# A decoder layer with latent attention and two expert stages on one core: low halves ahead of router steps, values copied first on ScalarE, unread products moved behind the attention loop, three normalisations on VectorE

## The reference, cut to what matters

```python
x = x + attn(layernorm(x))        # 8 heads, keys and values from 32 compressed features, softmax over 64 tokens
x = x + moe1(layernorm(x), ctx)   # router on ctx: best 2 of 8 experts per token, 128 -> 512 -> 128, relu
x = x + moe2(layernorm(x))        # 32 small experts, best 8 of 32, silu gate, and a shared expert
```

## Time and profile before

| | us |
|---|---|
| median of 3 runs (lowest to highest) | 756.46 (754.01 to 759.85) |
| the profiled execution's own time | 756.52 |
| its span, first to last instruction | 754.8 |
| PE busy in the span | 669.3 (89%) |
| DVE busy | 552.5 (73%) |
| POOL busy | 345.7 (46%) |
| ACT busy | 353.1 (47%) |

### The profile page before, as it was taken

The page is one execution under the profiler, slowest core; times in us unless marked ns, Lnnn a source line. Parts: engine busy times, 40 slices in busy tenths (PEclk is TensorE's granted clock), DMA queues, the critical chain, the costliest instruction groups (busy, mean ns, idle before and its releaser), DMA issues.

```text
span 754.8 us, 11001 instructions
## 1 busy us (share of the span) xinstructions
PE 669.3 (89%) x3456; PEld 475.5 (63%) x3456; DVE 552.5 (73%) x1318; ACT 353.1 (47%) x628; POOL 345.7 (46%) x386
## 2 busy tenths in 40 slices
PE   6868999999708999999992988999999999999997
PEld 5535666666506777777771755666666666666664
DVE  4367877779517999999964786777868695958564
ACT  3844666655204666666663533444343424353221
POOL 5111377778867999999957324040312213000000
PEclk9967999999958999999997898999999999999999
DMA  9900300000023466666311293354555545444442
GB/s 227 366 11 0 92 30 29 29 29 34 38 77 88 127 206 193 179 188 193 113 56 45 59 207 87 90 154 109 132 112 138 129 112 132 111 130 112 124 116 58
DMA packets 73816, 84.14 MB, mean 111 GB/s; under 512 B 15057, under 2 KB 42683, under 8 KB 73758
## 3 DMA queue, kind: packets, MB, share of 16 engines
q1 hardware_dynamic: 68536, 74.93, 36.4%
q0 software_dynamic: 4096, 8.40, 3.8%
q10 hardware_dynamic: 1126, 0.11, 0.1%
HBM read 64.48 MB, written 18.87 MB: 110 GB/s over the span
## 4 chain that ended last, share of the span: by engine, by line
PE 57%; POOL 18%; DVE 11%; issue 7%; ACT 4%; DMA 2%; another core or an unknown queue 0%; SPq 0%; POOLq 0%; ACTq 0%; DVEq 0%
PE pair_banks L1625 15%; POOL h1h L586 7%; PE bank L1408 7%; PE bank L1410 6%; PE bank L1409 6%; POOL W2l L571 4%; PE pair_banks L1315 4%; PE score_banks L1410 3%; PE score_banks L1408 3%; PE score_banks L1409 3%; POOL W2h L566 3%; PE bank L1447 2%; PE pair_banks L1493 2%; POOL x_sorted L544 2%; PE bank L1467 2%
## 5 line engine op out<-in xcount | busy, mean ns | idle before, releaser
L865 ACT ACTIVATE r_s<-bank 128x512 f32<-128x512 f32 x136 | 81.1, 598 | 160.7 <-PE bank L1410 150.8
L1625 PE MATMUL pair_banks<-t_s,Dn 128*128 128x512 f32 x272 | 138.6, 595 | 0.0
L1150 DVE TENSOR_TENSOR h1l<-r,h1h 128x512 fp32r<-128x512 f32 x92 | 113.4, 1251 | 16.2 <-POOL h1h L586 16.2
L1408 PE MATMUL bank<-fxh,Gh 128*128 128x512 f32 x136 | 97.6, 718 | 0.0
L1265 DVE TENSOR_TENSOR rc_s<-r_s,score_banks 128x512 f32<-128x512 f32 x90 | 61.5, 684 | 49.0 <-ACT r_s L865 39.5
L1278 DVE TENSOR_TENSOR t_s<-rc_s,bcb 128x512 f32<-128x512 f32 x128 | 87.4, 685 | 4.1 <-DMA bcb<-c_rows 2.6
L586 POOL TENSOR_SCALAR h1h<-r 128x512 fp32r<-128x512 f32 x92 | 73.8, 806 | 19.6 <-ACT r L816 17.3
L605 POOL TENSOR_TENSOR mvp<-mvp,meps 128x4 f32<-128x4 f32 x8 | 1.6, 197 | 172.4 <-DVE mvp L1188 172.4
L544 POOL DMA_INDIRECT x_sorted<-xsb,posi x64 | 64.2, 1003 | 31.9 <-DVE xsb L1077 19.8
L597 POOL DMA_INDIRECT yg<-y_sorted,posi x64 | 64.3, 1005 | 25.3 <-issue 18.4
L1625 PEld LDWEIGHTS pair_banks<-t_s,Dn 128*128 128x128 f32 x272 | 51.4, 190 | 14.7 <-issue 3.8
(11 more groups left out here) (286 smaller groups left out, 1611.4 us busy)
## 6 DMA issues: line engine op xcount, KB each, us to landing
bcb<-c_rows SPq DMA_DIRECT2D x128, 256.0 KB
wraw<-in_L_xattn_W SPq DMA_DIRECT2D x46, 256.0 KB, 2.9
x_sorted<-wraw SPq DMA_DIRECT2D x1, 5888.0 KB, 17.4
xg<-x_sorted SPq DMA_DIRECT2D x23, 256.0 KB, 3.4
y_sorted<-ysb SPq DMA_DIRECT2D x23, 256.0 KB, 3.0
ctxb<-in_ctx SPq DMA_DIRECT2D x8, 256.0 KB, 6.0
out<-x_all SPq DMA_DIRECT2D x8, 256.0 KB
x_all<-in_x SPq DMA_DIRECT2D x2, 512.0 KB, 5.2
```

The source lines that it names most:

```text
L865: act.activation(r_s[:, n % RB2, :], bank[n % 3][:, :], ACT.Silu).then_inc(F["act"], 1)
L1150: tt(h1l[:, n % NB1, :], r1[:, n % RB1, :], h1h[:, n % NB1, :].bitcast(F32), ALU.subtract)\
L1408: mm(dst, wh, xh, start=start, stop=False)
L1625: mm(bank[6][:, :], Dn[:, weights_of(p), :], t_s[:, n % TB2, :], start=(p == 0), stop=(p == NC2 - 1))\
```

## The change

1. `xl` (the low half `xnl`) is issued one pass earlier, behind that pass's `maximum` and ahead of the router; `first_of` is cut in three parts (`reach_top`, `first_key`, `only_first`) that are spread over more passes, and counts, bases, positions, blocks and weights come later. `kvlo` of block 1 moves to pass 0. `add_out_bias` moves one pass ahead.
2. On ACT `values` (the copy to `uS`) goes ahead of the copy to `ph` and the exponential.
3. The three unread products leave `output`. Behind the attention loop nine such products follow the landing of each of the last six tiles' scatters.
4. The normalisations of tiles 29, 30 and 31 go from POOL to DVE (`NV = NT - 3`).
5. The load of a block's biases counts on the semaphore of its weights (48 in place of 32).

```diff
-HEAD = dict(... xl=((-5, 0),), ...
+HEAD = dict(... xl=((-6, 0),), ...
+NV = NT - 3
@@ sync: load_expert
-                sp.dma_start(bcur[...], bT[:, ds(e, 1), :]).then_inc(s_b[b % BB], 16)
+                sp.dma_start(bcur[...], bT[:, ds(e, 1), :]).then_inc(s_w[b % WB], 16)
@@ gpsimd
                 m = n - LAG["norm"]
-                if 0 <= m < NT:
+                if 0 <= m < NV:
                     normalise_p(m)
@@ gpsimd: w_high
-                    pool.wait_ge(s_w[b % WB], 32 * (b // WB + 1))
+                    pool.wait_ge(s_w[b % WB], 48 * (b // WB + 1))
@@ scalar
+                if 0 <= n - LAG["u"] < NT:
+                    values(n - LAG["u"])
                 if 0 <= n - LAG["pT"] < NT:
                     transposed_p(n - LAG["pT"])
                 if 0 <= n - LAG["exp"] < NT:
                     exponent(n - LAG["exp"])
-                if n == 4:
+                if n == 5:
                     act.wait_ge(s_shift, 1)
                     act.activation(second[:, :, :], second[:, :, :], ACT.Exp).then_inc(s_exp1, 1)
-                if 0 <= n - LAG["u"] < NT:
-                    values(n - LAG["u"])
@@ vector: router1, by passes
                 if n == 3:
+                    router1_picked()
                     out_bias()
-                    router1_counts()
-                if n == 4:
+                if n == 5:
                     router1_bases()
-                if n == 5:
+                if n == 6:
                     router1_positions()
-                if n == 6:
+                if n == 8:
+                    router1_blocks()
+                if n == NT + 2:
                     router1_weights()
-                if n == 7:
-                    router1_blocks()
@@ vector: the loop
+                if n == 5:
+                    router1_counts()
                 if 0 <= o < NT:
                     residual1(o)
-                for step in head_steps(n, ("xl", "kvlo")):
-                    head(*step)
+                if n == 0:
+                    head("kvlo", 1, 0)
+                for name, j, part in head_steps(n, ("kvlo",)):
+                    if j != 1:
+                        head(name, j, part)
...
                     dve.reciprocal(rden[:, u % NP, :, :], ssum[:, u % NP, :, :]).then_inc(A["rden"], 1)
+                    if u >= NV:
+                        dve.wait_ge(A["rden"], u + 1)
+                        at = sm[:, u % NP, :].rearrange("p (h t) -> p h t", h=H)
+                        tt(at, at, rden[:, u % NP, :, :].to_broadcast([P, H, S]), ALU.mult).then_inc(A["pv"], 1)
...
                 if 0 <= n < NT:
                     maximum(n)
+                for step in head_steps(n, ("xl",)):
+                    head(*step)
                 statistics_rest(n)
                 router1(n)
-                if n % TPS == 1 and 5 <= n < NT + 5:
-                    add_out_bias((n - 5) // TPS)
+                if n % TPS == 0 and 4 <= n < NT + 4:
+                    add_out_bias((n - 4) // TPS)
@@ tensor: output
-                for c in range(3):
-                    mm(bank[0][:, (c + 1) * D:(c + 2) * D], tri[:, :], onesM[:, :], start=True, stop=True)
                 pe.wait_ge(A["uh"], n + 1)
@@ tensor: transposed_p
-                pe.wait_ge(A["p"], n + 1)
+                if n < NV:
+                    pe.wait_ge(A["p"], n + 1)
+                else:
+                    pe.wait_ge(A["pv"], n - NV + 1)
@@ tensor: the loop, and behind it
-                if n == 3:
+                if n == 4:
                     ranks()
-                if n == 4:
                     out_bias()
+            pe.wait_ge(A["x1"], NT)
+            for m in range(NT - 6, NT):
+                pe.wait_ge(s_sc[m % SC], 32 * (m // SC + 1))
+                for c in range(9):
+                    mm(bank[0][:, c % 3 * D:(c % 3 + 1) * D], tri[:, :], onesM[:, :], start=True, stop=True)
```

More of the change, by code:

```diff
@@ L53 @@
 EPS = 1e-5
-HEAD = dict(xn=((-12, 0), (-11, 1), (-9, 2), (-9, 3)), xT=((-7, 0),), xh=((-6, 0),), xl=((-5, 0),), kv=((-5, 0),),
+HEAD = dict(xn=((-12, 0), (-11, 1), (-9, 2), (-9, 3)), xT=((-7, 0),), xh=((-6, 0),), xl=((-6, 0),), kv=((-5, 0),),
             cq=((-5, 0),), kvS=((-4, 0),), cqS=((-3, 0),), kvlo=((-3, 0),),
@@ L299, in decoder_kernel @@
         s_w = [sem(f"expert_in{i}") for i in range(WB)]
-        s_b = [sem(f"expert_bias_in{i}") for i in range(BB)]
         s_xg = [sem(f"sorted_in{i}") for i in range(XB)]
@@ L318, in decoder_kernel @@
         A = {n: sem("at_" + n) for n in (
-            "xn xo xT xh xl kv_ps kvh kv cq_ps cq k_ps kst v_ps vh s_ps max sm exp sum rden p pT_ps ph "
+            "xn xo xT xh xl kv_ps kvh kv cq_ps cq k_ps kst v_ps vh s_ps max sm exp sum rden p pv pT_ps ph "
             "u_ps uh o_ps x1 bst mva eps rstd xs").split()}
@@ L412, in load_expert @@
                              W2[ds(e, 1), :, :].rearrange("e (c p) d -> p e c d", p=P)).then_inc(s_w[b % WB], 16)
-                sp.dma_start(bcur[:, b % BB, :].unsqueeze(1), bT[:, ds(e, 1), :]).then_inc(s_b[b % BB], 16)
+                sp.dma_start(bcur[:, b % BB, :].unsqueeze(1), bT[:, ds(e, 1), :]).then_inc(s_w[b % WB], 16)
             def load_sorted(b):
@@ L811, in _ @@
                 if c == 0:
-                    act.wait_ge(s_b[b % BB], 16 * (b // BB + 1))
+                    act.wait_ge(s_w[b % WB], 48 * (b // WB + 1))
                 act.wait_ge(B["up"], n + 1)
@@ L954, in _, with reach_top, first_key, only_first @@
             rev_b = rev[:, :].unsqueeze(1).to_broadcast([P, NT, E1])
-            def first_of(dst, values, top, k):
+            def reach_top(dst, values, top):
                 ch.done(dve.tensor_reduce(top[:, :, :], values, AX.X, ALU.max))
                 ch.done(tt(dst[:, :, :], values, top[:, :, :].to_broadcast([P, NT, E1]), ALU.is_equal))
+            def first_key(dst, k):
                 ch.done(tt(dst[:, :, :], dst[:, :, :], rev_b, ALU.mult))
                 ch.done(dve.tensor_reduce(k[:, :, :], dst[:, :, :], AX.X, ALU.max))
+            def only_first(dst, k):
                 ch.done(tt(dst[:, :, :], dst[:, :, :], k[:, :, :].to_broadcast([P, NT, E1]), ALU.is_equal))
@@ L977, in router1_pick, with router1_picked @@
                 dve.wait_ge(s_lgt, 2)
-                first_of(pick, lgt[:, :, :], best, key)
+                reach_top(pick, lgt[:, :, :], best)
+                first_key(pick, key)
             def router1_pick2():
+                only_first(pick, key)
                 ch.done(dve.scalar_tensor_tensor(pick2[:, :, :], pick[:, :, :], -HUGE, lgt[:, :, :], ALU.mult, ALU.add))
-                first_of(pick2, pick2[:, :, :], second, key)
+                reach_top(pick2, pick2[:, :, :], second)
+            def router1_picked():
+                first_key(pick2, key)
+                only_first(pick2, key)
                 tt(lgt[:, :, :], pick[:, :, :], pick2[:, :, :], ALU.add).then_inc(s_picked, 1)
```

## The result

| | before | changed |
|---|---|---|
| median, us | 755.24 | 743.91 |
| lowest to highest (4 executions each) | 753.54 to 759.85 | 742.67 to 745.60 |
| ratio, 95% interval | 1 | 0.9835 (0.9804 to 0.9865) |
| profiled execution, us (span) | 756.52 (754.8) | 742.98 (741.3) |

The changed kernel is faster by 1.3 to 2.0%. It was timed twice more among the experiments, beside runs of the kernel before that had a median of 752.0 and 752.8: 735.0 and 736.8 us, ratios 0.9791 (0.9761 to 0.9821) and 0.9805 (0.9778 to 0.9832). The kernel before itself lay between 752.0 and 756.3 from one series of runs to the next, so between series only ratios are compared. I forecast 739.6, a ratio of 0.978.

What follows compares the result with a forecast made beforehand. PE was taken to set 4.73 us per pass to about pass 25, then POOL and DVE 3.99, with POOL's last scatter ending attention. Gains 4.5 + 8.7 + 2.5 + 1.2 = 16.9 us; 756.5 - 16.9 = 739.6, range 734 to 749.

Steps and rivals of the forecast that it cites:

- Start: Up to pass 9: `xnl` 3.6 us earlier, lost unread products in passes 6 to 8 give 0.9; gain 4.5 us.
- Passes 9 to 25: Mid-attention: four passes fall from 18.92 to 16.8 us; gain 8.7 us, bounds 12.1 and 3.1.
- So POOL is next, with DVE and PE close behind: Mid-attention, per four passes: POOL needs 15.96 us, DVE 14.1, PE some 14, so POOL bounds.
- the lower bound of four passes is 15.96 us: Mid-attention: POOL's two pairs of 7.98 us set the least time of four passes; 16.8 was taken.
- The clock: Sign in the changed profile: PE's clock should be 1.00 from 85 us on.
- The rival had it in every group: Attention: PE's clock falls in every group of passes, 18.8 us per group, 747.6 us; chance 0.18.
- The missed pause: Mid-attention: bias add misses POOL's pause each time, taking 2.2 us; 18.2 us per group, 745.2 us; chance 0.12.
- Tail: End of attention: three passes lose POOL's normalisation, 3.3 us, less 0.8 given back; gain 2.5 us, bounds 0 and 3.3.
- the 0.8: Tail of attention: 0.8 us given back because DVE takes three more instructions and keeps POOL out meanwhile.
- the prediction's bound: Tail: VectorE as first comer at the port holds GpSimd off up to 2.0 us; sum would be 740.8.
- First block: First expert block: PE kept warm saves 0.5 us on transposes, 0.7 on the product; gain 1.2, bounds -2.2 and 1.5.
- Behind the first block: Expert stages after attention: same instructions, only shifted; 0 us, and time gained or lost there would make the prediction wrong.

Runs made afterwards that it cites:

- u_order: Changed kernel with the old order of router steps, subtraction, low halves and bias add on VectorE and of ranks on TensorE; 744.45 us, ratio 0.9891.
- only_fill: Kernel before without its three unread products in each output, nothing else changed; 756.43 us, ratio 1.0061.
- kvbias: Changed kernel with keys' low halves right behind the maxima and the bias add moved behind the next pass's sums; 731.94 us, ratio 0.9736.
- u_act: Changed kernel with ScalarE's copy of the values last in a pass again; 751.54 us, ratio 0.9943.
- u_norm: Changed kernel with the last three normalisations back on GpSimd; 743.91 us, ratio 0.9814.
- u_fill: Changed kernel with the three unread products of each output put back on TensorE; 751.84 us, ratio 0.9949.
- kvfirst: Changed kernel with the keys' low halves right behind the maxima in a group's first pass, ahead of the bias add; 738.45 us, ratio 0.9758.
- experiment 2: Changed kernel with the last three normalisations back on GpSimd, run twice: 743.91 us (0.9814), then 739.42 (0.9833) beside the changed kernel's 736.83 (0.9805).
- u_norm5: Changed kernel with the last three normalisations back on GpSimd, repeated beside the changed kernel with more runs; 739.42 us, ratio 0.9833.
- experiment 7: Changed kernel with keys' low halves right behind the maxima and the bias add behind the next pass's sums; 731.94 us, ratio 0.9736.

## Why the prediction was right, and where it was not

The total (16.9 us forecast, 11.3, 17.0 and 16.0 between the medians of the three timings) and the sign were right, 743.9 lies inside the range, and so do the other two timings. The sum was right partly by luck, because two terms missed in opposite directions: the maxima of pass 25 stood at 152.41 where I had 152.5, with 2.9 us more won at the start, 1.0 ahead of it and 3.7 less behind it.

*Start: 4.5 forecast, 7.4 in the profile (7.4 again in both repeats, 45.70).* The wait of 5.46 us ahead of block 2 shrank to 3.38 and `xnl` came early, as argued: counted from the maxima of pass 1 by 3.6 us (9.43 to 5.80), the term of the sum, and from pass 1 to pass 9 the change gives 4.4 against the 4.5 forecast. The step that failed is the list of what moves: the low halves of block 1, which now stand ahead of the sums of pass 0 and so ahead of the maxima of pass 0, were priced nowhere. Before, VectorE waited 5.46 us for the scores of pass 0 with kvS queued behind them, and TensorE's keys in pass 1 waited for kvS and then ran at half clock (0.50 from 40 to 44 us). The distance from the maxima of pass 0 to those of pass 1 fell from 5.50 us (36.70 to 42.20) to 2.50 (35.67 to 38.17): the missing 3 us. The keys in pass 1 of the kernel before, then of the changed one:

```profile
39.04 0.74 PE L1447 MATMUL bank<-kvS,GA 128*97 128x512 f32 x1 [1.42 <-DVE kvS L1064]
```

```profile
36.34 0.47 PE L1470 MATMUL bank<-kvS,GA 128*97 128x512 f32 x1
```

`u_order` loses the whole start, so it belongs to the order.

*Passes 9 to 25: 8.7 forecast, 4.98 in the profile.* Right: the gain was there, TensorE's products stood in the pass, the wait for `uS` would have taken their place without ScalarE's reorder (`only_fill`: it did), and the bias add stayed free. Wrong: "So POOL is next, with DVE and PE close behind". POOL isn't next. I compared busy times of engines, and the chain through them was longer: 17.24 against 15.96. The step is "the lower bound of four passes is 15.96 us", from which I took 16.8; the group measured 17.23 to 17.28 in all profiles of the changed kernel. `kvbias`, which shortens the chain, does reach 16.71. Of the 3.8 us that are missing, 1.8 are this in four groups, 1.4 the clock behind pass 9 and 0.6 the wait in pass 25. The prediction named the reorder as needed, but had no figure for the pass without it: `u_act` stands 7.6 us over `u_norm`, which was run beside it and copies the values first.

*The clock.* My forecast said 1.00 from 85 us on. It was 0.50 (1.2 GHz) at 80 to 84 and 0.54 at 154 to 158, behind waits of 2.92 and 2.02 us for `kvS` in passes 9 and 25. The rival had it in every group; it fell in two, and never in the three between. Later it fell again, to 0.66 at 172 to 176 and 0.50 at 192 to 196. The four passes from 9 take 18.63 us instead of 17.3 by it: 1.4 us. Passes 25 to 31 take 25.38 instead of 24.01, of which 0.8 are the normalisations on VectorE.

*The missed pause.* In the changed kernel it never happened (add 0.66 to 0.69), but three neighbours show it: `u_act` median 1.83, `u_fill` up to 2.03, `kvfirst` 2.20. The price of 2.2 us for one add was right, and is the upper end. Wrong was what it needs, "the scores to be late by half a microsecond or more": 0.29 us did it in `kvfirst`. So the rival was nearer than I had it.

*Tail: 2.5 forecast, 3.5 in the profile, of which 3.1 are the normalisations; they cost 0.8 ahead of it.* So 2.3 net by experiment 2, and 2.6 by the medians. The 3 x 1.1 came out. So did the 0.8, but not for its reason: GpSimd isn't kept out, the first of the three stands on VectorE ahead of the maxima of pass 31, so that these come 1.11 us behind `rden` instead of 0.40 in `u_norm5`. The Trainium skill's rule in "SBUF — State Buffer" (section "SBUF: two separate sides"), that the first comer keeps the port for its whole instruction, would have cost 2.0 here by the prediction's bound. The tail is short by the full 3.1, so there is no such loss at the last scatters. That doesn't speak against the rule, for VectorE was not the first comer: each of the three began 0.05 to 0.07 us behind a scatter, and neither held the other. One of them, on VectorE then GpSimd:

```profile
180.58 0.69 DVE L1137 TENSOR_TENSOR sm<-sm,rden 128x512 f32<-128x512 f32 x1
```

```profile
180.53 1.03 POOL L544 DMA_INDIRECT x_sorted<-xsb,posi  x1 [0.68 <-DVE xsb L1089]
```

Where VectorE did come first, by 0.14 us, the trace agrees. In the last group of the kernel before, a second scatter took 1.38 us behind the bias add's beginning, where others take 0.95 to 0.97:

```profile
194.97 0.69 DVE L1053 TENSOR_TENSOR x_all<-x_all,obb 128x512 f32<-128x512 f32 x1
```

```profile
195.11 1.38 POOL L544 DMA_INDIRECT x_sorted<-xsb,posi  x1 [0.30 <-issue]
```

*First block: 1.2 forecast.* From the last scatter to the first product 7.0 to 7.2 us in every profile with the end products and 7.5 to 7.6 in the three without, and the product itself 0.50 to 0.56 instead of 0.80. That is the forecast, seen in profiles and not timed by a kernel of its own. How much of it reaches the end isn't shown: to the last `h1h` of the first MoE it is 167.7 to 168.8 us from the last scatter in the three without and 166.6 to 168.4 in the others.

*Behind the first block: 0 forecast, about 3 us lost in the first profile.* From the last scatter to the end of the span the changed kernel took 536.8, 532.4 and 529.9 us in its three profiles, `u_norm` 536.9 and `u_norm5` 528.8, with the same instructions there. So stretches of the same code differ by 8 us from execution to execution; the loss is of that size, and nothing ties it to the change. The profiles show where it arises: behind the last `h1h`, in the second MoE, where the rest takes 361.2 to 369.7 us in the fourteen profiles. It goes with one wait of TensorE for VectorE's `cw`, in the changed kernel then in `u_norm5`:

```profile
440.94 1.04 PE L1338 MATMUL pair_banks<-ident,cw 128*32 128x128 f32 x4 [4.56 <-DVE cw L1276]
```

```profile
439.35 0.61 PE L1338 MATMUL pair_banks<-ident,cw 128*32 128x128 f32 x4 [1.15 <-DVE cw L1276]
```

The five profiles with a wait of 3.95 us or more (the kernel before among them) take 366.8 to 369.7 there, the seven with 2.7 to 2.8 us 362.6 to 364.5, the two with 1.2 us 361.2 and 361.6. Why the wait differs is open, and so is the 2.4 us between the kernel before (367.1) and the changed one (369.5).

## What to carry to other kernels

When the unread or unneeded work in front of an instruction is taken out, first read what that instruction waits for underneath: here the products and the wait for a copy filled the same microsecond, and each edit alone was worth little or less than nothing. The next bound is found by following one value round the ring of engines and adding its waits, not by comparing the engines' busy times, which gave 16.0 us where the group took 17.2. And every edit that shifts a pass shifts VectorE's instructions against GpSimd's, where one can hold up the other: the same bias add cost 0.68 or 2.20 us by whether GpSimd's normalisation began 0.88 or 0.59 us behind it, so this distance has to be read in the trace of each version.

## What the hardware did that was not expected

The same wait of 2.92 us for kvS in pass 9 took the clock away in one profile and not in the other (TensorE's row in the changed kernel, then in `u_norm5`, and the window behind it there):

```profile
77.97 0.47 PE L1470 MATMUL bank<-kvS,GA 128*97 128x512 f32 x1 [2.92 <-DVE kvS L1076]
```

```profile
79.43 0.47 PE L1470 MATMUL bank<-kvS,GA 128*97 128x512 f32 x1 [2.92 <-DVE kvS L1076]
```

```profile
80.00:84.00 4.00, 3.63 (x30) 2.09 (x29) 3.06 (x11) 2.76 (x6) 3.01 (x3) 1.00 0.93 233
```

In the first the clock is 0.50 at 80 to 84, in the second 1.00, and from pass 9 to pass 13 it is 18.63 and 17.28 us. In the two repeats of the changed kernel it fell as in the first, and in `u_norm`, whose code is the same there, behind 2.94 us too. So the length of a wait alone doesn't say whether the clock falls, and one kernel's executions can differ by 1.4 us at such a place. The Trainium skill ("TensorE: Matmul & The Clock Gate", section "HAM oscillation — how this bites in real kernels") says that idle stretches of PE take the clock and that it has to be earned back. The trace agrees that it happens (0.50 at 80 to 84 in the changed kernel); it adds that the same stretch may or may not do it.

In `kvbias` the clock was at 0.50 from 156 to 164 us (the first half of it):

```profile
156.00:160.00 4.00, 4.00 (x27) 2.85 (x26) 3.93 (x10) 2.02 (x5) 3.47 (x5) 0.50 0.10 37
```

Two passes still took GpSimd's 7.99 us there (the scatters of experiment 7), as at full clock in the earlier trace rows: half clock cost nothing where TensorE wasn't waited for.
